# A two-layer attention, FFN and MoE kernel: five engines' orders by period replaced by whole-run orders over seven streams

## The reference, cut to what matters

```python
# x: (64, 128, 128); ctx: (64, 120, 128)
x = x + attn16(layernorm(x), ctx)   # q, k RMS-normed per head, softmax(q k / sqrt 8) v, projection
x = x + ffn(layernorm(x))           # quantise, w1 (ternary), depthwise conv over S, silu, quantise, w2 (ternary)
x = x + attn1(layernorm(x), ctx)    # one head of width 128; [x, attn] @ w2_w
x = x + moe(layernorm(x))           # 8 experts, capacity 2: K = 128 of 128 tokens, so every expert gets all
#   moe: a = softmax(x @ gate_w); out = sum_e a[:, e] * ((silu(x @ Wg[e]) * (x @ Wu[e])) @ Wd[e])
```

## Time and profile before

| | |
|---|---|
| median of three runs | 1228.7 us |
| span of the profiled execution | 1219.6 us, 9.1 us under the median |
| PE busy | 1100.5 us, 90% |
| DVE busy | 984.3 us, 81% |
| ACT busy | 826.6 us, 68% |
| POOL busy | 682.8 us, 56% |
| first MoE product | at 200.66 us |

### The profile page before, as it was taken

One profiled execution on the slowest core, in us unless ns is written; L12 is line 12 of the kernel. 1 busy time (PEld: TensorE's weight loads), 2 busy tenths in 40 slices (PEclk: granted clock), 3 DMA queues, 4 the chain that ended last, 5 costly groups with the idle time before them and its releaser, 6 DMA issues.

```text
span 1219.6 us, 27479 instructions
## 1 busy us (share of the span) xinstructions
PE 1100.5 (90%) x9891; PEld 789.6 (65%) x9891; DVE 984.3 (81%) x2728; ACT 826.6 (68%) x1685; POOL 682.8 (56%) x827
## 2 busy tenths in 40 slices
PE   1677778999999899999999999999999998989998
PEld 1544555766767676767757676767767675767775
DVE  3668787989899898989898898989898897877653
ACT  1255375878768686768778686868778686868655
POOL 3212134566565747566575748475575747375775
PEclk9688898999999999999999999999999999999999
DMA  6120212121312113121212112130212022011000
GB/s 207 30 55 20 55 36 56 35 47 38 62 38 56 36 34 56 35 53 32 62 38 57 36 38 53 35 64 21 62 38 60 22 35 48 22 23 26 18 10 9
DMA packets 151396, 53.63 MB, mean 44 GB/s; under 512 B 116832, under 2 KB 150624, under 8 KB 150880
## 3 DMA queue, kind: packets, MB, share of 16 engines
q1 hardware_dynamic: 149248, 47.82, 17.7%
q10 hardware_dynamic: 2016, 4.08, 0.9%
HBM read 24.73 MB, written 4.19 MB: 24 GB/s over the span
## 4 chain that ended last, share of the span: by engine, by line
PE 72%; DVE 12%; SPq 5%; POOL 4%; issue 2%; ACT 2%; DMA 1%; POOLq 0%; DVEq 0%; ACTq 0%
PE py L750 16%; PE pa L601 5%; SPq L444 4%; PE pa L568 4%; PE pg L740 4%; PE pu L740 3%; PE pg L742 3%; PE pg L741 3%; PE pu L741 3%; PE pu L742 3%; PE pa L591 3%; DVE q_st L1155 2%; PE pa L608 2%; PE pb L648 2%; POOL xn L921 2%
## 5 line engine op out<-in xcount | busy, mean ns | idle before, releaser
L962 POOL TENSOR_TENSOR moe<-moe 128x512 f32<-128x512 f32 x256 | 336.3, 1318 | 293.7 <-ACT moe L897 147.8
L750 PE MATMUL py<-wd_s,moe 128*128 128x128 f32 x1856 | 248.7, 278 | 3.9 <-POOL moe L962 3.7
L750 PEld LDWEIGHTS py<-wd_s,moe 128*128 128x128 f32 x1856 | 231.7, 192 | 21.7 <-issue 7.8
L883 ACT ACTIVATE tg<-pg 128x512 f32<-128x512 f32 x232 | 139.7, 602 | 104.7 <-PE pg L742 104.0
L1155 DVE TENSOR_REDUCE q_st<-pa 128x4 f16<-128x480 f32 x256 | 168.4, 658 | 34.8 <-PE pa L568 33.6
L1307 DVE SCALAR_TENSOR_TENSOR moe<-tg,pg 128x512 f32<-128x512 f32 x232 | 157.3, 678 | 32.1 <-ACT tg L883 30.1
L897 ACT ACTIVATE moe<-pu 128x512 f32<-128x512 f32 x232 | 140.4, 605 | 33.7 <-PE pu L742 31.8
L817 ACT ACTIVATE probs<-pa 120x512 f32<-120x512 f32 x256 | 139.8, 605 | 22.3 <-PE pa L591 22.0
L568 PE MATMUL pa<-kbd,qht 128*128 128x480 f16 x256 | 96.4, 377 | 30.7 <-DVE q_st L1155 26.4
L740 PE MATMUL pg<-x4h,wg_h 128*128 128x512 f16 x232 | 88.6, 382 | 16.4 <-DVE moe L1307 16.4
L921 POOL TENSOR_SCALAR xn<-x,lnm,lnr 128x128 f32<-128x128 f32 x192 | 88.3, 473 | 5.2
(11 more groups left out here) (198 smaller groups left out, 2514.4 us busy)
## 6 DMA issues: line engine op xcount, KB each, us to landing
kbd<-kht SPq DMA_DIRECT2D x512, 3.8 KB
xin<-in_x SPq DMA_DIRECT2D x16, 256.0 KB, 2.8
xres<-in_x SPq DMA_DIRECT2D x16, 256.0 KB, 3.0
out_x<-acc SPq DMA_DIRECT2D x16, 256.0 KB, 3.2
ctxt_a<-in_ctx_t SPq DMA_DIRECT2D x16, 240.0 KB, 2.7
ctxt_b<-in_ctx_t SPq DMA_DIRECT2D x16, 240.0 KB, 2.9
ctxn_b<-in_ctx SPq DMA_DIRECT2D x16, 240.0 KB, 3.6
wd_s<-in_wd ACTq DMA_DIRECT2D x1, 1024.0 KB, 9.5
```

Of the source, the lines that this page charges most:

```text
L750: mm = pe.matmul(moe_y(g, e)[:, j, :], hu[:, u % 3, j * S:(j + 1) * S], wd_s[:, u, :], start=(half == 0 and j == 0), stop=(half == 1), ski ...
L883: act.activation(tg[:, u % 2, :], moe_bank("g", g, u)[:, :], ACT.Tanh, scale=0.5 / WSCALE).then_inc(tg_done.sem, 1)
L962: pool.tensor_tensor(hu[:, u % 3, :], gw[:, u % 3, :], us[:, u % 3, :], ALU.mult)\
```

## The change

`TURNS` goes; `ORDER` holds for each engine one string for the whole run, over seven letters: w, n, a, b, d, c and a new m, the maxima, which were part of a (on PE and DVE; on SP, m is the load of the second half of `kbd`). `run` gives each letter's stage one list of steps over all 16 groups. So a stage may run ahead of the others by any distance. Each engine has a step list of its own, with finer steps: `taps` becomes `right` and `left`, `qkv` becomes q, k, v on PE and qb, kb, msq, msk on DVE, a layernorm on POOL becomes `roots` and `normalise`, k and q transposes and the two `kbd` loads are single steps on SP. Inside a step instructions are the same, of the same shapes. Waits that the period gave are written out (for example ACT's side product waits for `sum_done` of the group before). `SIZES` is 16 times 4, so tiling is unchanged. Unread products: 162, two or three at a time, ahead of 59 steps, all ahead of the first MoE product.

```diff
-UNREAD = {
-    "wna": {2: 12, 6: 2, 9: 2, 10: 2, 11: 1, 14: 1, 19: 1, 22: 1, 24: 1, 29: 1, 32: 1, 36: 1, 41: 1, 44: 1, 45: 2, 49: 1, 50: 1, 52: 1},
...
+UNREAD = {1: 2, 2: 3, 3: 3, 4: 3, 6: 3, 7: 3, 8: 3, 11: 3, 12: 3, 13: 3, 14: 3, 15: 3, 16: 3, 18: 3, 20: 1, 32: 3, ...
+TAIL = 3
...
-TURNS = {
-    "pe": {
-        "n": "nnnnnnn",
-        "wna": "wnnawwanaaaaanaaaaaaaaaaaaaaaaaaaanwaaaaaaaaaaaanaanaw",
...
+STAGES = "wnmabdc"
+ORDER = {
+    "sp": (
+        "annnnmnnnnnnnnnmnnnnannmnbbnnnbbnanmdbbnbnnbnnanmdbbnbnbcnnnanmdbbbbncnnnnamdnbbbbnnnmcadnnnbbbbnnncamdnnnbb",
...
-        def periods(eng, body):
-            body(0, None, None, None, None)
-            body(1, 0, None, None, None)
...
+        def run(engine, do, between=None):
+            todo = {stage: iter([(step, g) for g in (range(NG) if stage != "w" else (0,))
+                                 for step in steps_of(engine, stage, g)]) for stage in STAGES}
+            for at, stage in enumerate("".join(ORDER[engine])):
+                if between is not None:
+                    between(at)
+                step, g = next(todo[stage])
+                do[stage](*step, g)
...
+            if engine == "pe":
+                if stage == "a":
+                    each = [(name, t, c) for t in seqs
+                            for name, c in (("stacks", 0), ("scores", 0), ("scores", 1), ("values", 0), ("turn", 0))]
+                    return each + plain("ont proj")
...
+                if stage == "m":
+                    return [("max", t, c) for t in seqs for c in range(4)]
...
+            return plain({"w": "", "n": "xin ctxa kht qht ks kbd0", "m": "kbd1", "a": "xres", "d": "ctxb", "c": "out"}[stage])
```

More of the change, by code:

```diff
@@ L29 @@
 B, S, SC, D = 64, 128, 120, 128
-GB = 4
-NG = B // GB
+SIZES = 16 * (4,)
+GB = max(SIZES)
+NG = len(SIZES)
+FIRST = tuple(sum(SIZES[:g]) for g in range(NG))
 T = GB * S
@@ L352, in build_program @@
-        n_steps = ["ln1", "xn1t", "qkv", "rms", "rms_k", "rms_q", "qkht"]
-        a_steps = [("max", 0, c) for c in range(4)]
-        a_steps.append(("stacks", 0))
-        for t in range(GB):
-            steps = [("scores", t, 0), ("max", t + 1, 0), ("scores", t, 1), ("values", t, 0), ("max", t + 1, 1),
-                     ("values", t, 1), ("max", t + 1, 2), ("max", t + 1, 3), ("turn", t), ("stacks", t + 1)]
-            a_steps += [step for step in steps if not (step[0] in ("max", "stacks") and step[1] == GB)]
@@ L359, in build_program @@
-        a_steps += ["ont", "proj"]
-        b_steps = ["ln2", "quant", "xit"]
-        for k in range(KB + 1):
-            steps = [("taps", k - 1), ("fc1", k), ("silu", k - 1)]
-            b_steps += [step for step in steps if 0 <= step[1] < KB]
-        b_steps += [(name, t) for t in range(GB) for name in ("h2t", "hit")] + ["fc2"]
-        d_steps = ["ln3", "xn3t", "bf", "s1", "p1n", "p1t", "oc", "fused", "ln4", "xn4t", "gate"]
-        c_steps = []
-        for u in range(NU):
-            c_steps += [("g", u), ("u", u)] + ([("d", u - 2)] if u >= 2 else [])
@@ L377, in build_program @@
-        for t in range(GB):
-            split[("turn", t)] = [("rden", t), ("turn", t)]
-            split[("h2t", t)] = [("h2t", t), ("clip", t), ("scale", t)]
-        dve_steps = {stage: [part for step in stage_steps[stage] for part in split.get(step, [step])]
-                     for stage in stage_steps}
-        engine_steps = {"dve": dve_steps, "pe": stage_steps, "act": stage_steps, "pool": stage_steps, "sp": stage_steps}
-        def run_turns(engine, n, a, b, d, c, do_w, do_n, do_a, do_b, do_d, do_c, between=None):
-            stage_steps = engine_steps[engine]
-            groups = {"w": 0 if n == 1 else None, "n": n, "a": a, "b": b, "d": d, "c": c}
-            kind = "".join(stage for stage in groups if groups[stage] is not None)
-            do = {"w": do_w, "n": do_n, "a": do_a, "b": do_b, "d": do_d, "c": do_c}
-            steps = {stage: iter(stage_steps[stage]) for stage in groups}
-            for at, stage in enumerate(TURNS[engine][kind]):
+            return g > 0
@@ new lines, in do_n, with load_part, do_m @@
+                    load_part(g, 0)
+            def load_part(g, half):
+                part = slice(0, first_half(g)) if half == 0 else slice(first_half(g), size(g))
+                for h in range(H):
+                    rows = slice(h * HD, (h + 1) * HD)
+                    sp.dma_start(kbd[rows, part, h, :], kht[rows, part, 0:SC]).then_inc(kbd_in[half][h // HQ].sem, 16)
+            def do_m(name, t, c, g):
+                sp.wait_ge(kht_in.sem, kht_in.at(g, 16))
+                if g == 0:
+                    sp.wait_ge(kbd_clear.sem, 1)
+                if later(g):
+                    sp.wait_ge(max_ps.sem, max_ps.at(g - 1, 4 * size(g - 1)))
+                load_part(g, 1)
@@ L683, in do_d @@
                         pe.wait_ge(w_lo.sem, 3)
-                if step in d_read:
-                    take(BANK["d"], d_read[step], g)
+                take(BANK["d"], d_read[step], g)
                 if step == "xn3t":
-                    for j in range(GB):
+                    for j in seqs:
                         mm = pe.transpose(pd[:, j * S:(j + 1) * S], xn3[:, j, :], id_f[:, :])
@@ L1304, in do_c @@
                 if what == "u":
                     dve.wait_ge(tg_done.sem, tg_done.at(g, u + 1))
-                    dve.scalar_tensor_tensor(out=gw[:, u % 3, :], in0=tg[:, u % 2, :], scalar=1.0, in1=moe_bank("g", g, u)[:, :],
-                                             op0=ALU.add, op1=ALU.mult).then_inc(gw_done.sem, 1)
-                elif what == "d" and u % 2 and u // 2 not in SIDE:
+                    dve.scalar_tensor_tensor(out=gw[:, u % 3, 0:wide], in0=tg[:, u % 2, 0:wide], scalar=1.0,
+                                             in1=moe_bank("g", g, u)[:, 0:wide], op0=ALU.add, op1=ALU.mult)\
+                       .then_inc(gw_done.sem, 1)
+                else:
```

908 lines of the change are left out of this document (482 added, 426 removed).

## The result

| | before | after | forecast |
|---|---|---|---|
| median of 5 runs, us | 1229.22 (1226.46 to 1233.49) | 1240.79 (1235.92 to 1241.86) | 1200.6 |
| ratio, 95% interval | 1 | 1.0085 [1.006, 1.0111] | 0.977 |
| span of the profiled execution, us | 1219.6 | 1239.9 | 1191.5 |
| first MoE product at | 200.7 | 193.4 | 197 |
| from there to the end, us | 1018.9 | 1046.5 | 994.5 |

The forecast was wrong in its direction. The last two lines say where: the start gained 7.3 us, more than forecast, and everything behind the first MoE product lost 27.6 us where a gain of 24.4 was expected.

A forecast was written before the change was run, and what follows sets the result against it. The prediction took PE to bound the middle and chains of waits to hold the start. Span 1219.6 − 23.4 − 3.7 − 1 = 1191.5 us, with 9.1 outside it 1200.6 us; range 1180 to 1232.

The forecast's parts named there:

- Step 1: Middle: of 33.4 us of PE waits where periods meet, 10 stay under the new order; gain 23.4 us.
- the seam: Middle: the place where one period meets the next, with PE's two big waits, 1.32 and 0.97 us.
- Step 2: Start, group 0's way to its first maxima: new order costs time, first `stacks` at 69.2 not 56.13, +13 us.
- Step 3: Start, from first `stacks` to first MoE product: DVE 82% filled, product at 197 us, gain 3.7 us.
- with the clock back: Start: DVE filled to 88%, first MoE product at 188, full PE clock saving 10 us more; 1176 us, chance 0.05.
- Step 4: The end of the kernel: same stream, same banks; gain 1 us, bounds ±3.
- The slower rival: Middle: DVE becomes the bound, its instructions put ahead of ones PE needs sooner; 1251 us, 1238 with half; chance 0.13.

The follow-up runs named there:

- e1: Changed kernel with POOL's MoE product replaced from the second group on by a power step of nearly its length that hardly reads; 1198.1 us, ratio 0.9762.
- e2: Kernel before the change with POOL's MoE product replaced from the second group on by a power step that hardly reads; 1220.6 us, ratio 0.9933.
- e10: Changed kernel with all its work, only VectorE's and POOL's strings in another order, heeding both POOL and TensorE's waits; 1203.2 us, ratio 0.9813.
- e3: Changed kernel without any of its unread products; 1254.8 us, ratio 1.0224 to the kernel before.
- e5: Changed kernel with only VectorE's string in another order, steps on SBUF alone moved away from POOL's products; 1225.3 us, ratio 0.9996.

## Why the prediction was wrong, by its steps

*Step 1, the middle: this is the one that failed.* It said 33.4 us of waits go and 10 stay, gain 23.4; measured were 50.6 us of waits and 70.8 us a group, over the 68 that the prediction named as the sign against this step. The waits at the seam, once a period at one place, did go. But the step took every instruction "in the durations that steps have" before, and the durations changed with the order. 70 us of standing still fell on an engine that I had at 91% (VectorE was busy for 90% of the time from 300 to 1000 us, and 38% of the last chain, before 12%), which the step put at nothing. With the cause taken out (e1 against e2) the gain behind the first MoE product is 18.8 us against 24.4 for steps 1 and 4 together: so its count of the orders was right in kind, and three quarters of it in size. With all work kept, e10 has 10.7 of it.

*Step 2, group 0's start.* The normalisation started at 24.18 (forecast 23.7) but took 5.96 us, not 1.75, since VectorE made the low parts of the MoE weights beside it:

```profile
24.14 2.28 DVE L1135 SCALAR_TENSOR_TENSOR wg_l<-h,wg_h 128x2048 f16<-128x2048 f32 x1
26.34 2.28 DVE L1135 SCALAR_TENSOR_TENSOR wu_l<-moe,wu_h 128x2048 f16<-128x2048 f32 x1
```

```profile
24.18 5.96 POOL L955 TENSOR_SCALAR xn<-xin,lnm,lnr 128x128 f32<-128x128 f32 x4
```

The same effect, here with POOL as the one that stands still. I had written that these casts "fall in this wait and cost nothing"; they cost 4.2 us. `kht` was issued at 42.73 (38.4), the fourth maximum ran at 71.86 (67.8), the first `stacks` at 73.51 (69.2).

*Step 3, to the first MoE product.* 119.9 us from the first `stacks` where 128 were forecast; the granted clock was 1.00 and not 0.90, and VectorE was busy for 103 us of it (86%; 82% forecast). The clock is that of the case "with the clock back", which I had given 0.05 and left out of the sum; the rest of that case, a first MoE product some 10 us ahead of 188, did not come. By e3 the start would be later than the old one without the unread products (207.8 against 200.7), so its gain hangs on them. That step 2's delay and step 3's gain come out near the forecast together is in part luck: each missed by 4 to 8 us, in opposite directions.

*Step 4, the end,* was not separated from the middle.

*The slower rival* had the right place, VectorE as the bound of the middle, and a price near the result (1238 with half of it), by luck. Its mechanism, steps placed ahead of what TensorE needs, is not the main one here: e1 leaves the order as it is and 31 to 35 us go. It did rule in e5.

## What to carry to other kernels

When an order changes and the instructions don't, their durations still may. Before pricing waits, list which of VectorE's instructions have all their tensors in SBUF (here reductions, statistics, reciprocals and one-column instructions did not matter) and which of POOL's full-width instructions will run beside them; here each meeting cost the one that came second nearly all that the other had left. An old order that keeps them apart, as here, is worth something that no sum of durations shows. Here sparse stretches of TensorE at the start were worth filling: by e3, 14 us.

## What the runs showed of the hardware

- In the nine traces in which POOL's product is whole, 510 VectorE instructions with only SBUF tensors and over one column (reductions, statistics and reciprocals left out) began with at least 0.3 us left of a POOL instruction of 512 columns or more: 499 were stretched, in the median by what POOL had left less 0.14 us. Of 6485 others (instructions with a PSUM input, reductions, statistics, reciprocals) none was. Nor was any of 221 `tensor_scalar` of one column. Here an instruction is measured against the lower quarter of its like in all twelve traces.
- POOL's power step doesn't shut VectorE out: in e1, 90 of VectorE's SBUF instructions and 11 of one column began with 0.3 us or more of one left, and none was stretched. The same holds for the power step of four columns that every kernel has (`lnr<-lnv,half`, 1.02 us): none of 385 in twelve traces. The Trainium skill's rule cited above, taken by its words (the whole of a POOL instruction that reads SBUF), would have stretched many of them, those with two SBUF inputs. The step takes 1.2 us for 5 columns, so most of it may be no access to SBUF; that is my reading, not shown.
- `am<-am` was once stretched to 3.7 us. It lies over three of POOL's instructions that follow each other without a gap, and ends with the last of them:

```profile
353.18 3.71 DVE L1242 TENSOR_SCALAR am<-am 128x4 f32<-128x4 f32 x1
```

```profile
353.15 1.27 POOL L1034 TENSOR_TENSOR x2b<-x,a2b_s 128x512 f32<-128x512 f32 x1
354.37 1.27 POOL L1000 TENSOR_TENSOR moe<-moe 128x512 f32<-128x512 f32 x1
355.60 1.27 POOL L991 TENSOR_TENSOR xres_b<-xres,bp_s 128x512 f32<-128x512 f32 x1
```

- So VectorE did not get in between two POOL instructions; that it never can is not shown. What the 26 us of standing still that e10 still has would give back stays open.
